# A four-layer graph kernel: an order of its own for the last slot

## The reference, cut to what matters

```python
def _L1_gnn_ref(h, causal_mask, W_lang, W_grav, W_V, W_O, gate_logit, log_sigma):
    z_l = einsum('bnd,ed->bne', h, W_lang)
    z_g = einsum('bnd,ed->bne', h, W_grav)
    v = einsum('bnd,ed->bne', h, W_V)
    zn = z_l / maximum(norm(z_l, axis=-1, keepdims=True), EPS)
    A_l = maximum(einsum('bnd,bmd->bnm', zn, zn), 0.0) * not_eye
    sq = sum(z_g * z_g, axis=-1, keepdims=True)
    d2 = maximum(sq + swapaxes(sq, -1, -2) - 2.0 * einsum('bnd,bmd->bnm', z_g, z_g), 0.0)
    A_g = exp(-d2 / (2.0 * sigma * sigma)) * not_eye
    K_l = _row_stochastic_causal(A_l, causal_mask)    # mask with adj, divide by row sums
    K_g = _row_stochastic_causal(A_g, causal_mask)
    K = w_l * K_l + (1.0 - w_l) * K_g
    return einsum('bnd,ed->bne', einsum('bnm,bmd->bnd', K, v), W_O)

x = _layernorm(x + _L0_gnn_ref(...))
x = _layernorm(x + _L1_gnn_ref(x, adj, ...))
x = _layernorm(x + _L2_gnn_ref(...))
x = _layernorm(x + _L1_gnn_ref(x, adj, ...))     # layer 4, the same form
```

## Time and profile before

| | |
|---|---|
| median of 3 runs | 2059.3 us (2059.19 to 2059.37) |
| the profiled execution | 2057.45 us |
| its span, first to last instruction | 2055.6 us |
| TensorE busy in it | 2013.2 us (98%) |
| DVE busy | 1645.6 us (80%) |
| ACT busy | 1061.9 us (52%) |
| POOL busy | 149.2 us (7%) |
| mean granted TensorE clock | 0.995 |

### The profile page before, as it was taken

How to read it: one execution, slowest core, us unless ns; L and a number is a source line. 1 busy time by engine, 2 the same in 40 slices (tenths; PEclk the granted TensorE clock), 3 DMA queues, 4 the chain that set the end, 5 groups by cost and what they waited for, 6 DMA issues and landing times.

```text
span 2055.6 us, 34568 instructions
## 1 busy us (share of the span) xinstructions
PE 2013.2 (98%) x13436; PEld 1830.5 (89%) x13436; DVE 1645.6 (80%) x4398; ACT 1061.9 (52%) x1965; POOL 149.2 (7%) x198
## 2 busy tenths in 40 slices
PE   6899999999999999999999999999999999999997
PEld 6789899999999989999999998999999999999996
DVE  5577888888788888878888887888878888787885
ACT  5444546455454555546455554645545464554643
POOL 0000010000101000010100001000000100001010
PEclk9999999999999999999999999999999999999998
DMA  4100010000001000010000001001000100001000
GB/s 144 51 6 17 1 42 1 11 32 11 32 1 41 2 11 32 1 42 1 24 19 11 32 1 42 1 11 31 11 32 1 42 1 11 32 1 42 1 22 21
DMA packets 23652, 44.69 MB, mean 22 GB/s; under 512 B 2624, under 2 KB 2880, under 8 KB 23488
## 3 DMA queue, kind: packets, MB, share of 16 engines
q1 hardware_dynamic: 23488, 42.48, 6.0%
HBM read 25.70 MB, written 16.78 MB: 21 GB/s over the span
## 4 chain that ended last, share of the span: by engine, by line
PE 93%; DVE 3%; ACT 2%; issue 1%; DMA 0%; SPq 0%; POOL 0%; POOLq 0%; ACTq 0%; DVEq 0%
PE psum L499 12%; PE psum L484 12%; PE psum L334 11%; PE psum L473 8%; PE psum L474 7%; PE psum L342 7%; PE psum L424 6%; PE psum L530 6%; PE psum L338 5%; PE psum L524 4%; PE psum L525 4%; PE psum L428 3%; PE psum L511 3%; DVE vs L981 2%; PE psum L579 1%; PE psum L585 1%
## 5 line engine op out<-in xcount | busy, mean ns | idle before, releaser
L981 DVE TENSOR_TENSOR zs<-psum,zs 128x512 fp32r<-128x512 f32 (+1 forms) x456 | 265.9, 610 | 87.0 <-ACT zs L697 84.0
L697 ACT ACTIVATE zs<-psum 128x512 fp32r<-128x512 f32 (+1 forms) x456 | 233.4, 536 | 162.9 <-PE psum L484 106.3
L499 PE MATMUL psum<-xs,zs 128*128 128x256 f32 x2048 | 275.7, 285 | 0.0
L499 PEld LDWEIGHTS psum<-xs,zs 128*128 128x128 f32 x2048 | 258.0, 191 | 2.4
L697 ACT ACTIVATE vs<-psum 128x512 fp32r<-128x512 f32 x128 | 76.6, 599 | 301.4 <-PE psum L530 299.5
L342 PE MATMUL psum<-ident,full 128*128 128x128 f32 x1220 | 168.5, 275 | 15.9 <-DMA full<-in_L_gnn_wk_dram 5.0
L697 ACT ACTIVATE full<-psum 128x512 f32<-128x512 f32 x160 | 95.2, 595 | 154.0 <-PE psum L342 94.7
L342 PEld LDWEIGHTS psum<-ident,full 128*128 128x128 f32 x1220 | 139.3, 141 | 38.5 <-DVE full L1076 17.6
L424 PE MATMUL psum<-vs,zs 128*128 128x512 f32 x512 | 141.2, 397 | 1.6 <-ACT vs L697 1.6
L334 PE MATMUL psum<-vs,zs 128*128 128x512 f32 x512 | 140.7, 397 | 0.7 <-ACT zs L697 0.7
L1058 DVE BATCH_NORM_STATS2 stats<-full 128x6 f32<-128x512 f32 x192 | 129.9, 690 | 4.4
(11 more groups left out here) (192 smaller groups left out, 5195.4 us busy)
## 6 DMA issues: line engine op xcount, KB each, us to landing
full<-in_x_dram SPq DMA_DIRECT2D x32, 512.0 KB, 3.5
out_dram<-full SPq DMA_DIRECT2D x32, 512.0 KB, 2.9
full<-in_L_gnn_W_lang_dram SPq DMA_DIRECT2D x2, 1024.0 KB, 5.5
full<-in_L_gnn_W_grav_dram SPq DMA_DIRECT2D x2, 1024.0 KB, 8.2
full<-in_L_gnn_W_O_dram SPq DMA_DIRECT2D x2, 1024.0 KB, 5.8
full<-in_L_gnn_W_V_dram SPq DMA_DIRECT2D x2, 1024.0 KB, 5.5
full<-in_adj_dram SPq DMA_DIRECT2D x1, 256.0 KB, 2.6
bias_row<-in_L_gnn_bias_dram SPq DMA_DIRECT2D x1, 256.0 KB, 7.1
```

The lines of the kernel that those rows point to most:

```text
L499: last = mm(halves(bank)[:, n, :], y[:, e, n * P:(n + 1) * P], HTH[s][:, e, :], start=(y is ZH[s][kind] and e == 0 and n == 0), stop=(y is ...
L697: return nc.scalar.activation(dst, src, func, **kw)
L981: return tt(dst, src, plain(hi), ALU.subtract)
```

## The change

A function `last_slot` takes the place of the last call of `seam_slot` and of `tail`, on every engine. Stream 1's second value tile is computed first, in its own bank 2. The norms' transposes then come behind the second `symmetrise`, without a wait for values. The first value tile is computed last, in bank 0 of stream 0, which is through by then (`home=r`). The statistics of stream 0 stand ahead of the last split of Z. The last layer norm of stream 1 goes tile by tile: ACT normalises tile 0 and DVE tile 1, POOL has a power for each tile, and SP has a store for each tile.

```diff
 SyncE
-            for s in range(2):
-                store(s, TURNS - 1)
-            for s in range(2):
-                sp.wait_ge(stored[s], 16 * TURNS)
+            store(0, TURNS - 1)
+            first = (TURNS * 2 - 1) * NT
+            sp.wait_ge(last_ready[1], TURNS * 2 - 1)
+            sp.dma_start(out_tiles[:, first, :], CUR[1][:, 0, :]).then_inc(stored[1], 16)
+            sp.wait_ge(cur1_ready[1], TURNS * 2 + 1)
+            sp.dma_start(out_tiles[:, first + 1, :], CUR[1][:, 1, :]).then_inc(stored[1], 16)
+            sp.wait_ge(stored[0], 16 * TURNS)
+            sp.wait_ge(stored[1], 16 * (TURNS + 1))
 TensorE
-            def values_head(s, l, n):
+            def values_head(s, l, n, home=None):
+                bank = psum[s if home is None else home][:, 2 * n, :]
...
-            def norm_rows(s, j, l):
+            def norm_rows(s, j, l, values_in_bank=True):
                 pe.wait_ge(mat_ready[s], j * 4 + (2 * l + 1))
-                pe.wait_ge(vl_ready[s], j * 4 + (2 * l + 1))
+                if values_in_bank:
+                    pe.wait_ge(vl_ready[s], j * 4 + (2 * l + 1))
...
-            def tail(r, j):
+            def last_slot(s, j, r):
...
+                symmetrise(s, j, 1, 0)
+                values_head(s, 1, 1)
+                symmetrise(s, j, 1, 1)
+                norm_rows(s, j, 1, values_in_bank=False)
+                values_tail(s, 1, 1)
+                pe.wait_ge(res_ready[r], j * 6 + 5)
+                values_head(s, 1, 0, home=r)
+                values_tail(s, 1, 0, home=r)
+                transpose_k(s, j, 1)
+                mix_values(s, j, 1)
 ScalarE, in its last_slot
+                copy_gram(s, j, 1, 0)
+                copy_gram(s, j, 1, 1)
+                last_normalise(r, j)
+                gauss(s, j, 1)
+                split_v(s, j, 1, 1, turn=0)
+                mix_gauss(s, j, 1)
+                split_v(s, j, 1, 0, turn=1, home=r)
+                split_kt(s, j, 1)
+                last_tile(s, j, 0)
 VectorE
+            def last_tile_var(s, j, n):
+                dve.wait_ge(res_ready[s], j * 6 + (4 + n + 1))
+                own_later(s, nc.vector.bn_stats(last_stats[s][:, n, :], CUR[s][:, n, :]))
+                own_wait(s)
+                own(s, j, nc.vector.bn_aggr(last_mv[s][:, n, :], last_stats[s][:, n, :]))
+                ts(last_veps[s][:, n:n + 1], last_mv[s][:, n, 1:2], EPS_LN, None,
+                   ALU.add).then_inc(last_var_ready[s], 1)
...
+            def last_tile(s, j, n):
+                dve.wait_ge(last_rstd_ready[s], j + (n + 1))
+                ts(CUR[s][:, n, :], CUR[s][:, n, :], last_mv[s][:, n, 0:1], last_rstd[s][:, n:n + 1], ALU.subtract,
+                   ALU.mult).then_inc(cur1_ready[s], 1)
 GpSimd
-            seam_slot(1, e, 1, 0, e, None)
-            last_inverse_std(1, e)
+            inverse_norm(1, e, 1)
+            last_tile_inverse_std(1, e, 0)
+            last_tile_inverse_std(1, e, 1)
```

More of the change, by code:

```diff
@@ L519, in values_terms, with values_tail @@
                 return [(HTH[s][:, d, cols], HTL[s][:, d, cols], wh[:, d, :], wl[:, d, :]) for d in range(FT)]
-            def values_head(s, l, n):
+            def values_head(s, l, n, home=None):
+                bank = psum[s if home is None else home][:, 2 * n, :]
                 for i, (xh, xl, wh, wl) in enumerate(values_terms(s, l, n)):
-                    mm(psum[s][:, 2 * n, :], xh, wh, start=(i == 0), stop=False)
-                    mm(psum[s][:, 2 * n, :], xh, wl, start=False, stop=False)
-            def values_tail(s, l, n):
+                    mm(bank, xh, wh, start=(i == 0), stop=False)
+                    mm(bank, xh, wl, start=False, stop=False)
+            def values_tail(s, l, n, home=None):
+                bank = psum[s if home is None else home][:, 2 * n, :]
                 for i, (xh, xl, wh, wl) in enumerate(values_terms(s, l, n)):
-                    last = mm(psum[s][:, 2 * n, :], xl, wh, start=False, stop=(i == FT - 1))
+                    last = mm(bank, xl, wh, start=False, stop=(i == FT - 1))
                 last.then_inc(v_done[s], 1)
-            def norm_rows(s, j, l):
+            def norm_rows(s, j, l, values_in_bank=True):
                 pe.wait_ge(mat_ready[s], j * 4 + (2 * l + 1))
-                pe.wait_ge(vl_ready[s], j * 4 + (2 * l + 1))
+                if values_in_bank:
+                    pe.wait_ge(vl_ready[s], j * 4 + (2 * l + 1))
                 for t in range(NT):
@@ L689, in _ @@
             middle_slot(0, e, 1, 1, e)
-            seam_slot(1, e, 1, 0, e, None)
-            tail(1, e)
+            last_slot(1, e, 0)
         @block.scalar
@@ L794, in last_normalise @@
                         bias=last_shift[s][:, n:n + 1]).then_inc(last_ready[s], 1)
+            def last_tile(s, j, n):
+                act.wait_ge(last_shift_ready[s], j + 1)
+                run(CUR[s][:, n, :], CUR[s][:, n, :], ACT.Identity, scale=last_rstd[s][:, n:n + 1],
+                    bias=last_shift[s][:, n:n + 1]).then_inc(last_ready[s], 1)
             def split_xt(s, j, l):
@@ L808, in copy_gram, with split_v @@
                 run(M[s][:, (1, 3)[kind], :], psum[s][:, (3, 1)[kind], :]).then_inc(gram_copied[s], 1)
-            def split_v(s, j, l, n):
-                act.wait_ge(v_done[s], j * 4 + (2 * l + n + 1))
-                run(VH[s][:, n, :], psum[s][:, 2 * n, :]).then_inc(vh_ready[s], 1)
+            def split_v(s, j, l, n, turn=None, home=None):
+                act.wait_ge(v_done[s], j * 4 + (2 * l + (n if turn is None else turn) + 1))
+                run(VH[s][:, n, :], psum[s if home is None else home][:, 2 * n, :]).then_inc(vh_ready[s], 1)
             def gauss(s, j, l):
@@ L938, in seam_slot, with last_slot @@
                     split_xt(r, jn, 0)
-            def tail(r, j):
+            def last_slot(s, j, r):
                 gauss(r, j, 1)
                 mix_gauss(r, j, 1)
+                split_z(s, j, 1, 0, 0)
+                split_z(s, j, 1, 0, 1)
                 split_kt(r, j, 1)
+                split_z(s, j, 1, 1, 0)
+                split_z(s, j, 1, 1, 1)
+                copy_gram(s, j, 1, 0)
+                copy_gram(s, j, 1, 1)
                 last_normalise(r, j)
+                gauss(s, j, 1)
[4 more added lines that the diff above has]
+                last_tile(s, j, 0)
             start()
@@ L1173, in split_z, with split_v @@
                     ZS[s][:, 4 * kind + part, :]).then_inc(zl_ready[s], 1)
-            def split_v(s, j, l, n):
-                dve.wait_ge(vh_ready[s], j * 4 + (2 * l + n + 1))
-                low(VL[s][:, n, :], psum[s][:, 2 * n, :], VH[s][:, n, :]).then_inc(vl_ready[s], 1)
+            def split_v(s, j, l, n, turn=None, home=None):
+                dve.wait_ge(vh_ready[s], j * 4 + (2 * l + (n if turn is None else turn) + 1))
+                low(VL[s][:, n, :], psum[s if home is None else home][:, 2 * n, :],
+                    VH[s][:, n, :]).then_inc(vl_ready[s], 1)
             def spread(s, kind):
@@ L1391, in tail @@
                 last_stats_var(r, j)
+                split_z(s, j, 1, 1, 1)
                 last_norm_shift(r, j)
+                squares_l(s, j, 1)
+                spread_l(s, j, 1)
+                gauss_start(s, j, 1)
+                cosine_start(s, j, 1)
+                kernel_rows(s, j, 1)
+                kernel_mix(s, j, 1)
+                split_v(s, j, 1, 1, turn=0)
+                split_v(s, j, 1, 0, turn=1, home=r)
+                split_kt(s, j, 1)
+                add_kv(s, j, 1, 0)
+                last_tile_var(s, j, 0)
+                add_kv(s, j, 1, 1)
+                last_tile_shift(s, j, 0)
+                last_tile_var(s, j, 1)
+                last_tile(s, j, 1)
             start()
```

19 lines of the change are left out of this document (18 added, 1 removed).

## The result

The changed kernel takes 2048.66 us (median), against 2059.19 for the kernel before in the same comparison: a ratio of 0.9952 with a 95% interval of 0.9938 to 0.9966. (One of its five runs took 4012.83 us and is left out of the ratio; the other four took 2046.87 to 2049.73.) The 2059.19 is the median of five runs: the three that the prediction had (2059.19 to 2059.37) and two that it had not, 2057.30 and 2057.47 us; against those two the changed kernel is 8.7 us faster. In a second comparison it took 2048.93 against 2057.09, ratio 0.9962 (0.9948 to 0.9976).

What follows compares the result with a forecast made beforehand. TensorE was taken as busy nearly all the time, with the last slot's tail a single chain behind a late K. Savings of 4.3 + 2.5 + 1.3 + 0.3 = 8.4 us from 2059.3 gave 2050.9 us, range 2049.7 to 2053.3.

Steps and rivals of the forecast that it cites:

- (4): Twelve products with K in the tail: full clock after a short gap, 2.97 us instead of 5.51, 2.5 us less.
- (5): Last layer norm by tile: second add to the store's issue takes 3.65 us instead of 4.98, 1.3 us less.
- (3): First value tile, now last, is late next; products with K start at 2037.6 instead of 2041.96, 4.3 us less.
- (6): Final store of 256 KB instead of 512: 0.3 us less from issue to end, bounds 0 and 1.4.
- (1): TensorE's norm transposes move behind the second symmetrise; DVE's spread copies come 0.9 or 0.6 us early, no wait added.
- (2): K's chain in the last slot: K ready at 2035.7 instead of 2040.2, some 0.4 us before TensorE can use it.
- the clock did not fall in the short gap: Rival: the clock falls in TensorE's gap of about 1 us, costing 2.5 us; 2052.9 us, chance 0.11.
- K's wait stay: Rival: hand-offs lengthen K's chain, TensorE still waits after the values; only 3.2 us less, 2056.1 us, chance 0.06.
- TensorE stand at the norms: Rival: late spread copies stall TensorE at the norm transposes, making it 1.3 us slower, 2060.6 us; chance 0.03.

Runs made afterwards that it cites:

- e1: The changed kernel with its new order kept but the last layer norm and store for both tiles together as before; 2050.96 us, ratio 0.9971, last slot 19.86 us.
- e4: The kernel before with 16 spare products on TensorE in the gap ahead of K's transposes; 2054.97 us, ratio 0.9990, last slot 23.83 us.
- e2: The kernel before, in its old order, with the tile-wise last layer norm and two stores; 2054.69 us, ratio 0.9988, last slot 23.79 us.
- w_before: The kernel before with 45 spare products on TensorE in gaps of the first 90 us; 2053.94 us, ratio 0.9988.
- w_after: The changed kernel with 45 spare products on TensorE in gaps near the start; 2046.06 us, ratio 0.9948.
- a_again: The changed kernel run once more with no edit; 2047.31 to 2049.92 us in five runs.

## Why the prediction was wrong, and where it was right

In the last slot it was right, term by term (times counted from the slot's start; the boundary between (4) and (5) is the point at which the second add could start, 2047.47 before and 2041.86 after, where it was held until 2042.31):

| term | predicted | measured | from |
|---|---|---|---|
| (3) products with K start earlier | 4.3 | 4.15 | 12.86 us into the slot before, 8.71 after |
| (4) full clock | 2.5 | 2.5 | 5.51 to 3.0 (e1, with nothing between the adds, has 3.02); e4 shows the cause |
| (5) layer norm by tile | 1.3 | 1.37 | 4.98 to 3.61 |
| (6) store | 0.3 | 0.72 | 3.15 to 2.43 |
| sum | 8.4 | 8.74 | 26.50 to 17.76 |

(1) The norms find their copies, with 0.93 us in hand at the tighter place, where 0.9 was reckoned. (2) K is ready 6.71 us into the slot; 6.6 was reckoned. The store is the one mis-sized term. The nearest row was a load of 256 KB, 2.6 us; the store of that size lands after 2.0, and the last store of before had landed after 2.7, less than the median of 2.9. The estimate by the page of the Trainium skill, DMA: Bandwidth & Descriptors, Anatomy of one DMA, had 0.6 for it and was nearer, though the page's formula, for transfers issued by GpSimd (2.6 us for 256 KB), is itself too slow for these.

Three smaller slips change nothing. The parts of (5) add up to 3.61 us, not 3.65. The range's own bounds put its lower end at 2049.8. And the first half store was not quite over when the second was issued at 2045.47: the GB/s of the changed kernel from 2043 to 2048, in slices of 0.125 us, show its bytes until about 2045.75, and the second's only from 2046.25 on:

```profile
GB/s 0 0 0 0 0 0 0 0 0 0 0 0 0 0 0 147 459 344 442 377 312 17 0 0 0 0 131 475 344 442 360 328 17 0 0 0 0 0 0 0
```

Of the rivals, the clock did not fall in the short gap in any of the eight profiles with the new order, each with a gap of 1.06 or 1.07 us and four products behind it at 1.16 or 1.17. In the changed kernel neither did K's wait stay, nor did TensorE stand at the norms.

The step that failed is in the sum's last sentences: "The median of the runs is 1.85 us above the profiled execution, so the forecast for it is 2059.3 - 8.4". It took the three runs of before, 2059.19 to 2059.37, for the kernel's time, and the 1.85 us for a constant. They were not. The two further runs of before in the same comparison took 2057.30 and 2057.47 us, and the kernel before took 2057.09 (21 runs), 2057.53 (16 runs) and 2057.21 us (9 runs) in later comparisons, on three chips, with single runs from 2054.30 to 2061.87. From 2057.2 the same 8.74 us give 2048.5, where 2048.66 and 2048.93 were measured. The profiled execution, 2057.45 us, was the better base: with the 8.4 as forecast it gives the prediction's own 2049.05. The range had no term for this, though the rows that bear on it were in use: the earlier trace rows show two gaps of nearly one length with different ends, and even behind one gap the moment of the fall moves between executions. In e2's profile the clock falls behind the second of them too, 2.33 us as in the earlier trace rows, but after the first four products, and from these to layer 2 it takes 32.41 us where the profile of before has 33.16:

```profile
68.42 1.19 PE L338 MATMUL psum<-xs 128*128 128x512 f32 x4 [2.33 <-DVE vs L993]
69.45 1.78 PE L338 MATMUL psum<-xs,vs 128*128 128x512 f32 x4
```

That the start accounts for some of the spread is shown by w_before and w_after (3 us, and half the spread). Why three runs of the kernel before stood at 2059.2 to 2059.4 is not shown: they have neither a profile nor a granted clock on record.

## What to carry to other kernels

A median of three runs that agree to 0.2 us can still stand 2 us off, when single runs of the kernel spread over 4 us; a range for a change of 8 us needs a term for that, and a stretch that both profiles share, measured from one instruction to the end, shows a change far more sharply than the total does. The wait of 4 us in front of TensorE cost twice, once as time and once as clock: filling it with products that nobody reads gave 2.7 us back with the wait still there. When work is moved up in front of a queue that must not stop, look at who feeds it: a third of a microsecond in hand was enough, and the statistics left in their old place would have cost 1.3 us.

## What the runs showed of the hardware that I had not expected

The length of a gap of about 2 us does not tell whether the clock falls: behind 2.02 us it fell in the changed kernel's profile and not in a_again's; behind 1.90 us in w_after's and not in w_before's. Behind 2.33 us it fell in the profile of before ahead of the first product (0.50 from 68 us on) and in e2's only after the first four. With 26 transposes ahead of them, the first eight products took 2.14 us instead of 3.59. And the windows of the kernel before give a granted clock of 1.00 in its first 60 us, though eight products at 12.17 us took 3.78 us there, as slow as products at 0.50 elsewhere (four at 69.14 us took 2.07): at the start, durations tell more than the clock's column. POOL's power of one column takes 0.55 us, of two 0.69.
